# A block of exact row maxima as a short loop, the middle batches written out, and a maximum over partitions taken through TensorE

## The chip, the cores and the metric

The kernel runs on one core of one Trainium2 chip. The metric is the device time in microseconds (us) of one execution. A profile is one further execution, recorded by the hardware profiler; its span runs from the first to the last instruction.

## What is computed

One transformer layer in float32 accuracy: attention with rotary embedding over 4 batches of 1024 tokens with 256 channels and 16 heads of 16, then a mixture of 8 experts of which each token uses 2. Cut to what matters here:

```python
x = x + attn(layernorm(x))        # B=4, L=1024, E=256, H=16, HD=16
#   q, k = rope(x @ Wq.T + bq), rope(x @ Wk.T + bk);  v = x @ Wv.T + bv
#   softmax(q k^T / 4) v @ Wo.T + bo
x = x + ffn(layernorm(x))
#   nf = rmsnorm(x) in bf16; top 2 of 8 logits, softmax over the two
#   p1 = nf @ mlp1; act = min(g,7) * sigmoid(1.702 g) * (clip(lin)+1)
#   combined = sum over experts of weight * (act @ mlp2)
```

The softmax needs protection from overflow. The kernel bounds every score of a batch by the largest norm of a query times the largest norm of a key. If the bound is small, the exponential is taken without a shift. If it is large, a block of code first computes the exact maximum of each row of scores and the shift is the negative of that. With the inputs used here the bound stays small: in the profile the block is jumped over in each of the 4 batches.

## The kernel before

The kernel is written for the five engines by hand: each engine has its own instruction stream, and semaphores join them. An engine's sequencer reads the stream, does branches, waits and register arithmetic itself and queues the rest. PE is TensorE, DVE is VectorE, ACT is ScalarE, POOL is GpSimd, SP is SyncE, which here only issues DMAs.

Work is cut into 4 batches (`b`), each of 2 chunks (`n`) of 512 query tokens. A chunk of attention is 32 steps (`s`): 4 groups of 4 heads (`g`) times 8 tiles of 128 keys (`kt`). A step is two pairs of score matmuls into `S` (line 673), two exponentials on ACT into `probs` (line 804) and 4 pairs of matmuls into `OP` (line 687). The scores of the next step are issued before the values of this one, but not across the end of a batch.

Other work is put beside the steps by a table of due times in half steps: `PREP` prepares the next batch's chunk (normalisation `stats1`, `xn`; transposes `xT`; projections `qk`, `v`; rotation; the squared norms `length`), `POST` finishes the attention of the chunk before and does the gating, `EXPERTS` does 16 half experts (`up`, `tanh`, `hidden`, `down`). Most TensorE work of the table goes through the one PSUM bank `D`: a stage in the list `FILLS` waits until the reader of the bank's last content has read it (`read_of`), fills the bank and counts `d_full`; the reader then waits for that count. `down` uses the same bank and waits in the same manner.

Per batch there is one check of the bound. `length` leaves maxima over tokens in `nsq` (line 970). At half step 36 of the second chunk stage `guard` runs: DVE reduces `nsq` to `nsq2`, one value per partition for queries and one for keys (line 974), and POOL takes their maxima over the 128 partitions into `nsqa` by `partition_all_reduce` (line 868). At half step 44 stage `flag` multiplies the two and writes `exact_flag` (lines 977 and 979). For batch 0 the same happens in a head, before any attention, with the stages in the order of a list, `HEAD`, and with four PSUM banks in turn.

Between batches each of SP, PE and DVE runs `turn(b)`: it waits for the flag, loads it into a register (lines 426, 706, 1153), and jumps over the exact block if it is 0 (lines 511, 707, 1154) and then over nothing at a second branch (lines 524, 727, 1166), behind which semaphores are set that the block would have set. On PE the block is 128 score groups written out, each a wait and two matmuls with their weight loads; on DVE it is 128 pairs of a wait and a reduction. On PE `turn` ends with the first scores of the batch. On SP in front of it, in the last step of the batch, stand the seven loads of a group's `Qs` and `Ks`, and behind it, in step 0, the load of the next `X` (line 438), that of `X1s` (line 447) and the write of `O`. In batch 0 `turn` itself issues 14 loads of `Qs` and `Ks`.

The batches: `body(0)` is written out, batches 1 and 2 are the two passes of a hardware loop over one code, `body(3)` is written out, then a tail without attention. ACT issues the load of an expert's weights (line 796) once per expert, behind a `tanh`, so the starts of line 796 mark how far the table has come.

## Time and profile before

| | us |
|---|---|
| median of 3 runs | 1203.12 |
| lowest, highest | 1199.26, 1204.91 |
| profiled execution | 1205.98 |
| its span | 1204.1 |
| its mean granted TensorE clock | 0.906 of full speed |

In the rows of the trace a time in square brackets is the idle time of the engine ahead of the instruction and what ended it; "issue" there means that the profile shows nothing the engine waited for. A name with a q (PEldq, SPq) is an engine's sequencer. MODIFY_POOL_CONFIG is an instruction that `partition_all_reduce` brings along, as does the first ordinary POOL operation behind it.

### The profile page before, as it was taken

The numbers are of one execution on the slowest core, as the hardware profiler recorded it, in microseconds if no ns is written. First come the engines' busy times: TensorE is split into PE (matmuls) and PEld (weight loads), VectorE is DVE, ScalarE is ACT, GpSimd is POOL, SyncE is SP. The second block draws the span as 40 slices with busy tenths as digits, with TensorE's granted clock in tenths as the row PEclk, the third lists the DMA queues.
The fourth block names the chain that finished last, engine by engine and source line by source line (L and its number), as shares of the span: only waits on it lengthen the run. The fifth ranks groups of instructions, "written<-read, shape, count | busy, mean of one in ns | idle before, by whom it ended". The sixth has DMA issues, their size and how long they took to land.

```text
span 1204.1 us, 18696 instructions
## 1 busy us (share of the span) xinstructions
PE 974.9 (81%) x5241; PEld 414.1 (34%) x5313; DVE 828.1 (69%) x1622; ACT 697.5 (58%) x905; POOL 424.8 (35%) x360
## 2 busy tenths in 40 slices
PE   4608897889679897987778997888799999996564
PEld 1302222233233443333233343323343344344243
DVE  5732102669658797677676799586867897797797
ACT  2318895856448574765448665675567676771232
POOL 2413303433244333533235333542232333233243
PEclk9858998989889999988799898999989899997587
DMA  4254454324424252434413345352534353421011
GB/s 150 74 108 79 102 104 99 88 74 97 116 59 130 77 117 82 102 96 95 119 37 103 98 108 118 71 128 67 114 86 107 97 125 82 101 76 58 31 53 31
DMA packets 80001, 110.08 MB, mean 91 GB/s; under 512 B 22523, under 2 KB 56707, under 8 KB 76803
## 3 DMA queue, kind: packets, MB, share of 16 engines
q1 hardware_dynamic: 61444, 83.47, 29.9%
q10 hardware_dynamic: 18432, 25.17, 7.0%
q8 instruction: 52, 0.85, 0.3%
q14 instruction: 73, 0.59, 0.2%
HBM read 82.89 MB, written 25.69 MB: 90 GB/s over the span
## 4 chain that ended last, share of the span: by engine, by line
PE 49%; DVE 25%; issue 13%; ACT 4%; DMA 3%; POOL 2%; SPq 2%; another core or an unknown queue 1%; DVEq 0%; ACTq 0%; POOLq 0%
PE OP L687 13%; PE S L673 12%; PE D L659 8%; DVE th_sb L1103 3%; DVE act_sb L1108 3%; PE A L642 3%; PE D L569 3%; PE D L586 3%; PE BB L642 3%; DVE acc L1098 2%; DVE g_sb L1086 2%; DVE l_sb L1088 2%; DMA X<-in_x 2%; DVE xn L946 2%; ACT probs L804 2%
## 5 line engine op out<-in xcount | busy, mean ns | idle before, releaser
L804 ACT ACTIVATE probs<-S 128x1024 f32<-128x1024 f32 x512 | 511.8, 1022 | 256.2 <-PE S L673 253.4
L673 PE MATMUL S<-Qs,Ks 98*128 98x512 bf16 x1024 | 312.4, 399 | 61.8 <-issue 23.0
L687 PE MATMUL OP<-probs,V 128*17 128x512 f32 x2048 | 280.1, 620 | 2.7 <-ACT O L813 2.7
L891 POOL TENSOR_TENSOR act_lo<-act_sb,act_hi 128x512 fp32r<-128x512 f32 x128 | 165.5, 1293 | 212.3 <-DVE act_hi L1114 152.4
L673 PEld LDWEIGHTS S<-Qs,Ks 98*128 98x128 bf16 x1024 | 81.4, 101 | 249.0 <-ACT probs L804 98.7
L659 PE MATMUL D<-W,act_hi 128*128 128x256 f32 x448 | 135.6, 333 | 29.5 <-DVE Vn L986 16.2
L1098 DVE SCALAR_TENSOR_TENSOR acc<-D,combh,acc 128x256 f32<-128x256 f32 x224 | 97.1, 475 | 82.5 <-PE D L659 82.1
L1103 DVE SCALAR_TENSOR_TENSOR th_sb<-th_sb,g_sb 128x512 f32<-128x512 f32 x128 | 129.6, 1012 | 0.7 <-ACT th_sb L780 0.7
L885 POOL TENSOR_SCALAR W<-W2b 128x512 fp32r<-128x512 bf16 x64 | 45.4, 709 | 217.4 <-PE D L659 212.1
L1108 DVE SCALAR_TENSOR_TENSOR act_sb<-l_sb,th_sb 128x512 f32<-128x512 f32 x128 | 107.2, 837 | 16.7 <-POOL act_lo L891 12.2
L659 PE MATMUL D<-W,act_lo 128*128 128x256 f32 x448 | 116.3, 290 | 0.0
L780 ACT ACTIVATE th_sb<-g_sb 128x512 f32<-128x512 f32 x128 | 80.0, 625 | 51.4 <-DVE g_sb L1086 50.7
L659 PEld LDWEIGHTS D<-W,act_hi 128*128 128x128 f32 x448 | 88.5, 198 | 56.4 <-issue 24.7
L642 PE MATMUL A<-nfT,W 128*128 128x512 bf16 x185 | 66.2, 418 | 34.5 <-DVE g_sb L1086 24.9
L1086 DVE TENSOR_SCALAR g_sb<-A,b1f 128x512 f32<-128x512 f32 x120 | 89.3, 744 | 4.2 <-PE A L642 4.2
L659 PEld LDWEIGHTS D<-W,act_lo 128*128 128x128 f32 x448 | 89.0, 199 | 2.3
L1088 DVE TENSOR_SCALAR l_sb<-BB,b1f 128x512 f32<-128x512 f32 x120 | 89.0, 742 | 0.5
L642 PE MATMUL BB<-nfT,W 128*128 128x512 bf16 x239 | 77.6, 408 | 0.4
L687 PEld LDWEIGHTS OP<-probs,V 128*17 128x17 f32 x2048 | 34.3, 96 | 116.5 <-issue 87.2
L569 PE MATMUL D<-xnT,wqk_sb 128*128 128x512 f32 x108 | 53.4, 618 | 11.4 <-DVE acc L1098 8.3
L858 POOL TENSOR_TENSOR sw<-sw,sin_sb 128x512 f32<-128x512 f32 x32 | 43.2, 1349 | 49.0 <-DVE sw L953 48.9
L1114 DVE CAST act_hi<-act_sb 128x512 fp32r<-128x512 f32 x112 | 51.7, 461 | 4.2
(136 smaller groups left out, 1016.7 us busy)
## 6 DMA issues: line engine op xcount, KB each, us to landing
W<-in_w ACTq DMA_DIRECT2D x64, 256.0 KB, 2.7
Ks<-k_scr SPq DMA_DIRECT2D x32, 384.0 KB
W2b<-in_w ACTq DMA_DIRECT2D x64, 128.0 KB, 2.7
Ks<-k_scr SPq DMA_DIRECT2D x32, 256.0 KB
o_scr<-O SPq DMA_DIRECT2D x32, 256.0 KB, 4.5
q_scr<-parts SPq DMA_DIRECT2D x16, 384.0 KB, 3.1
k_scr<-parts SPq DMA_DIRECT2D x16, 384.0 KB, 2.6
Qs<-q_scr SPq DMA_DIRECT2D x32, 192.0 KB
```

The source lines that it names most:

```text
L569: last = mm(bank[:, :], wqk_sb[:, c, P * a:P * (a + 1)], xnT[:, c, :], start=c == 0, stop=c == CT - 1)
L642: last = mm(bank, W1[:, e % 2, c, FI * gl + P * it:FI * gl + P * (it + 1)], nfT[:, c, :], start=c == 0, stop=c == CT - 1)
L659: last = mm(bank[:, E * q:E * (q + 1)], part[:, e % 2, it, tok:tok + P], W2[:, e % 2, E * it:E * (it + 1)], start=k == 0, stop=k == 3)
L673: last = mm(S[:, j2, C * i:C * (i + 1)], Ks[0:SROWS + MROWS, g % 2, j, P * kt:P * (kt + 1)], Qs[0:SROWS + MROWS, g % 2, j, :], start=True, ...
L687: last = mm(OP[32 * j:32 * j + VW, :], V[:, kt, HG * g + j, :], probs[:, s % 2, C * j:C * (j + 1)], start=kt == 0, stop=kt == KT - 1)
L804: nc.scalar.activation(probs[:, s % 2, 2 * C * j2:2 * C * (j2 + 1)], S[:, j2, :], ACT.Exp, scale=SCALE).then_inc(exp_done, 1)
L891: tt(act_lo[:, e % 2, it, :], act_sb[:, a % 2, :], act_hi[:, e % 2, it, :].bitcast(FP32), ALU.subtract).then_inc(lo_s, 1)
L1086: v.tensor_scalar(g_sb[:, q, :], gate, b1f[:, e, 0, it:it + 1], LIMIT, ALU.add, ALU.min).then_inc(g_s, 1)
L1088: v.tensor_scalar(l_sb[:, q, :], linear, b1f[:, e, 1, it:it + 1], 1.0 - LIMIT, ALU.add, ALU.max).then_inc(l_s, 1)
L1098: v.scalar_tensor_tensor(acc[:, t, :], output[:, E * i:E * (i + 1)], combh[:, t, e:e + 1], acc[:, t, :], ALU.mult, ALU.add).then_inc(m2_ev, 1)
L1103: v.scalar_tensor_tensor(th_sb[:, q, :], th_sb[:, q, :], 1.0, g_sb[:, q, :], ALU.add, ALU.mult).then_inc(t1_s, 1)
L1108: v.scalar_tensor_tensor(act_sb[:, q, :], l_sb[:, q, :], 1.0 + LIMIT, th_sb[:, q, :], ALU.min, ALU.mult).then_inc(act_s, 1)
```

## The change

Three things. The exact block becomes loops in registers: on PE one loop of 4 passes for each group of heads, on DVE one of 16 passes for each chunk; the matmuls take their operands at an address from the loop's register. Batches 1 and 2 are written out instead of being passes of a hardware loop. The maximum over partitions is taken by two TensorE transposes of `nsq2` into the first row of a bank and one DVE reduction of 256 values: stage `gmax` (half step 36) holds the old DVE part of `guard`, `guard` moves to half step 39 and becomes a filling of the bank, `flag` moves from 44 to 41. `nsqa`, `bound` and `exact_flag` shrink to one partition.

```diff
-          "qk3": 30, ..., "v1": 42, "guard": 1, "flag": 8, ...
+          "qk3": 30, ..., "v1": 42, "gmax": 1, "guard": 4, "flag": 6, ...
-    place(PREP, h + AT["length"] + AT["guard"], ("guard", 0))
-    place(PREP, h + AT["length"] + AT["guard"] + AT["flag"], ("flag", 0))
+    for st in ("gmax", "guard", "flag"):
+        place(PREP, h + AT["length"] + AT[st], (st, 0))
-    HEAD += [("guard", 0, 1), ("flag", 0, 1)]
+    HEAD += [("gmax", 0, 1), ("guard", 0, 1), ("flag", 0, 1)]
-    FILLS = ("xT", "qk", "v", "length", "wo", "nfT", "logits", "combT", "b2")
+    FILLS = ("xT", "qk", "v", "length", "guard", "wo", "nfT", "logits", "combT", "b2")
...
             body(0, True, FILLED0)
-            with engine.Fori(1, B - 1) as b:
+            for b in range(1, B - 1):
                 body(b, True, FILLED1 + LOOP_FILLS * (b - 1))
             body(B - 1, False, FILLED3)
...
 # PE, read_of
+                        "guard": (nsqa_s, u // NCH + 1), ...
 # PE, stage
+                elif st == "guard" and n == NCH - 1:
+                    pe.wait_ge(nsq_s, bb + 1)
+                    for t in range(2):
+                        last = nc.tensor.transpose(bank[0:1, P * t:P * (t + 1)], nsq2[:, t:t + 1], ident[:, :])
+                    last.then_inc(d_full, 1)
 # PE, turn
-                            for j in range(HG):
+                            with pe.Fori(0, HG) as j:
                                 for t in range(TC):
-                                    i = 16 * (NG * n + g) + TC * j + t
-                                    if i >= 2:
-                                        wait_apart(pe, (ex_red, 128 * b + i - 1))
+                                    wait_apart(pe, (ex_red, 128 * b + 16 * (NG * n + g) + t + 1 + TC * j))
                                     for hf in range(2):
-                                        last = mm(S[:, i % 2, C * hf:C * (hf + 1)], Qs[0:SROWS, g % 2, j, P * t:P * (t + 1)],
-                                                  Ks[0:SROWS, g % 2, j, C * hf:C * (hf + 1)], start=True, stop=True)
+                                        last = mm(S[:, t % 2, C * hf:C * (hf + 1)],
+                                                  Qs[0:SROWS, g % 2, bass.ds(j, 1), P * t:P * (t + 1)].rearrange("k o t -> k (o t)"),
+                                                  Ks[0:SROWS, g % 2, bass.ds(j, 1), C * hf:C * (hf + 1)].rearrange("k o t -> k (o t)"),
+                                                  start=True, stop=True)
                                     last.then_inc(ex_mm, 1)
-                    wait_apart(pe, (ex_red, 128 * (b + 1)))
+                    wait_apart(pe, (ex_red, 128 * (b + 1) + 1))
 # POOL, stage
-                elif st == "guard" and n == NCH - 1:
-                    wait_apart(pool, (nsq_s, bb + 1))
-                    nc.gpsimd.partition_all_reduce(nsqa[:, :], nsq2[:, :], P, bass.bass_isa.ReduceOp.max).then_inc(nsqa_s, 1)
 # DVE, stage
-                elif st == "guard" and n == NCH - 1:
+                elif st == "gmax" and n == NCH - 1:
                     dve.wait_ge(nrm_red, 4 * (u + 1))
                     v.reduce_max(nsq2[:, :], nsq[:, :, :], AX_X).then_inc(nsq_s, 1)
+                elif st == "guard" and n == NCH - 1:
+                    dve.wait_ge(d_full, k + 1)
+                    v.reduce_max(nsqa[:, :], bank[0:1, 0:2 * P].rearrange("o (a p) -> o a p", a=2), AX_X).then_inc(nsqa_s, 1)
 # DVE, turn
-                    for i in range(128):
-                        n, g, j, t = i // 64, i // 16 % NG, i // TC % HG, i % TC
-                        wait_apart(dve, (ex_mm, 128 * b + i + 1))
-                        h = HG * g + j
-                        v.reduce_max(mx[:, TC * n + t, h:h + 1], S[:, i % 2, :], AX_X).then_inc(ex_red, 1)
+                    for n in range(NCH):
+                        with dve.Fori(0, H) as h:
+                            for t in range(TC):
+                                wait_apart(dve, (ex_mm, 128 * b + 64 * n + t + 1 + TC * h))
+                                v.reduce_max(mx[:, TC * n + t, bass.ds(h, 1)], S[:, t % 2, :], AX_X).then_inc(ex_red, 1)
```

The remaining lines count the fillings of bank `D` with one more per batch and start the semaphore `ex_red` at 1, so that the first waits of the loop have a positive value.

## Rows read from the trace of the kernel before

**Rows 1.** Page, parts 1, 3 and 4: engines; instruction fetches; chain by engine.
```profile
PE 974.9 (81%) x5241; PEld 414.1 (34%) x5313; DVE 828.1 (69%) x1622; ACT 697.5 (58%) x905; POOL 424.8 (35%) x360
...
q8 instruction: 52, 0.85, 0.3%
...
PE 49%; DVE 25%; issue 13%; ACT 4%; DMA 3%; POOL 2%; SPq 2%; another core or an unknown queue 1%; DVEq 0%; ACTq 0%; POOLq 0%
```

**Rows 2.** Chain in order of time, end of the head: start us, us, what.
```profile
68.82 5.82 issue
...
75.42 0.02 SPq L345
```

**Rows 3.** Line 345, waits on their own, 68 to 72 us: engine, count, ns, first to last start.
```profile
L345 SPq EVENT_SEMAPHORE  x2: 17/17/17, 69.0 to 71.1; - x2
```

**Rows 4.** Timeline around the check of batch 1's bound: start, us, engine, line, idle before.
```profile
260.29 0.37 POOL L868 PARTITION_ALL_REDUCE nsqa<-nsq  x1 [11.31 <-issue]
...
267.50 1.26 POOL L891 TENSOR_TENSOR act_lo<-act_sb,act_hi 128x512 fp32r<-128x512 f32 x1 [6.83 <-issue]
...
268.90 1.00 DVE L1108 SCALAR_TENSOR_TENSOR act_sb<-l_sb,th_sb 128x512 f32<-128x512 f32 x1 [3.26 <-POOL act_lo L891]
```

**Rows 5.** Line 796 in four stretches; the last two numbers are first and last start.
```profile
L796 ACTq DMA_DIRECT2D W<-in_w x3: 339/339/339, 403.8 to 426.0; - x3
L796 ACTq DMA_DIRECT2D W<-in_w x3: 334/334/334, 258.4 to 285.0; - x3
L796 ACTq DMA_DIRECT2D W<-in_w x3: 339/339/340, 536.1 to 565.7; - x3
L796 ACTq DMA_DIRECT2D W<-in_w x3: 339/339/339, 818.8 to 845.8; - x3
```

**Rows 6.** Lines 563 and 970, whole execution: count, ns least/median/most.
```profile
L563 PE MATMUL D<-ident,xn x52: 272/418/476, 9.9 to 753.0; 128*128 128x128 f32 x52
L970 DVE TENSOR_REDUCE nsq<-D x24: 684/692/693, 114.1 to 812.2; 128x1 f32<-128x512 f32 x24
```

**Rows 7.** Branches on the sequencers: count, ns least/median/most, first to last start.
```profile
L707 PEldq COMPARE_BRANCH  x4: 3901/6237/8002, 76.4 to 865.8; - x4
L377 PEldq COMPARE_BRANCH  x2: 76/2698/5320, 591.6 to 874.2; - x2
L1154 DVEq COMPARE_BRANCH  x4: 56/63/67, 76.4 to 868.5; - x4
L1166 DVEq COMPARE_BRANCH  x4: 55/55/55, 79.5 to 876.5; - x4
L511 SPq COMPARE_BRANCH  x4: 50/52/64, 76.4 to 869.9; - x4
```

**Rows 8.** Timeline at the three turns between batches, first scores, and DVE behind them.
```profile
313.72 1.86 PE L673 MATMUL S<-Qs,Ks 98*128 98x512 bf16 x4 [7.41 <-issue]
...
318.82 0.88 DVE L1098 SCALAR_TENSOR_TENSOR acc<-D,combh,acc 128x256 f32<-128x256 f32 x2 [10.09 <-PE D L659]
...
591.51 1.88 PE L673 MATMUL S<-Qs,Ks 98*128 98x512 bf16 x4 [4.66 <-issue]
...
597.13 1.03 PE L673 MATMUL S<-Qs,Ks 98*128 98x512 bf16 x2 [3.74 <-issue]
...
874.05 1.89 PE L673 MATMUL S<-Qs,Ks 98*128 98x512 bf16 x4 [7.17 <-issue]
```

**Rows 9.** Timeline, load of X behind the first and second turn and its first use.
```profile
310.04 0.43 SPq L438 DMA_DIRECT2D X<-in_x  x1
...
323.79 1.40 DVE L918 BATCH_NORM_STATS2 st<-X 128x6 f32<-128x256 f32 x4
...
596.30 0.43 SPq L438 DMA_DIRECT2D X<-in_x  x1
...
604.98 1.39 DVE L918 BATCH_NORM_STATS2 st<-X 128x6 f32<-128x256 f32 x4
```

**Rows 10.** Chain in order of time between the chunks of batch 1.
```profile
447.63 8.38 DMA X<-in_x
```

More of the change, by code:

```diff
@@ L127, in block_kernel @@
             HEAD += [("sum", *tile[0])]
-    HEAD += [("guard", 0, 1), ("flag", 0, 1)]
+    HEAD += [("gmax", 0, 1), ("guard", 0, 1), ("flag", 0, 1)]
     HEAD_BANKS = 4
-    FILLS = ("xT", "qk", "v", "length", "wo", "nfT", "logits", "combT", "b2")
-    PREP_FILLS = sum(st in FILLS for l in PREP.values() for st, _ in l)
+    FILLS = ("xT", "qk", "v", "length", "guard", "wo", "nfT", "logits", "combT", "b2")
+    PREP_FILLS = sum(st in FILLS and st != "guard" for l in PREP.values() for st, _ in l)
     POST_FILLS = sum(st in FILLS for l in POST.values() for st, _ in l)
@@ L159, in stages @@
                 k = (self.n, self.last, False)
-                if st in FILLS:
+                if st in FILLS and (st != "guard" or chunk == NCH - 1):
                     self.n, self.last = self.n + 1, (st, a, NCH * batch + chunk)
@@ L270, in block_kernel @@
         nsq2 = sb("nsq2", [P, 2], FP32)
-        nsqa = sb("nsqa", [P, 2], FP32)
-        bound = sb("bound", [P, 1], FP32)
-        exact_flag = sb("exact_flag", [P, B], INT32)
+        nsqa = sb("nsqa", [1, 2], FP32)
+        bound = sb("bound", [1, 1], FP32)
+        exact_flag = sb("exact_flag", [1, B], INT32)
         lgb = sb("lgb", [P, TC, NE], BF16)
@@ L345, in wait_apart @@
                 engine.sem_inc(passed, 1)
-        FILLED0 = NCH * PREP_FILLS
-        FILLED1 = FILLED0 + NCH * PREP_FILLS + POST_FILLS
-        LOOP_FILLS = NCH * (PREP_FILLS + POST_FILLS)
+        FILLED0 = NCH * PREP_FILLS + 1
+        FILLED1 = FILLED0 + NCH * PREP_FILLS + 1 + POST_FILLS
+        LOOP_FILLS = NCH * (PREP_FILLS + POST_FILLS) + 1
         FILLED3 = FILLED1 + 2 * LOOP_FILLS
@@ L547, in read_of @@
                 return {"xT": (xnT_s, 2 * u + a + 1), "qk": (qk_b, 4 * u + a + 1), "length": (nrm_red, 4 * u + a + 1),
-                        "v": (vn_s, 2 * u + a + 1), "wo": (x1_s, 2 * u + a + 1), "nfT": (nfT_s, u + 1),
+                        "guard": (nsqa_s, u // NCH + 1), "v": (vn_s, 2 * u + a + 1), "wo": (x1_s, 2 * u + a + 1), "nfT": (nfT_s, u + 1),
                         "down": (m2_ev, 2 * (NF * u + a + 1)), "logits": (gating, GATING * u + 1), "combT": (combT_s, u + 1), "b2": (acc_s, 2 * u + a + 1)}[st]
@@ L553, in stage @@
                 u = NCH * bb + n
-                if st in FILLS and filling[1]:
+                if st in FILLS and filling[1] and (st != "guard" or n == NCH - 1):
                     pe.wait_ge(*read_of(*filling[1]))
@@ L1168, in turn @@
                     dve.sem_inc(ex_red, 128)
+            dve.sem_inc(ex_red, 1)
             v.memset(half_pow[:, :], -0.5).then_inc(c_set, 1)
```

4 rows, old and new, of the table AT are left out of this document.

## The prediction

> **What bounds the kernel now.** Read the page first. TensorE is busy 81% of the span and the chain that ended last lies on it for 49%, on DVE for 25%; 13% is "issue", time in which an engine stood still and the profile shows no work that it waited for [rows 1]. An 81% busy engine with a chain that hops to DVE is no place for large gains by less work, so the 13% is where to look. The change touches three places, and each is a stall of this kind. The chain in order of time shows the first, at the end of the head: 5.82 us of "issue", from 68.82 on, ahead of the maximum over partitions [rows 2]. The timeline shows the same in the check of each later batch's bound, only in the middle of running work: POOL is still for 11.31 us ahead of its 0.37 us instruction and for another 6.83 us behind it, and DVE and then TensorE come to stand behind POOL [rows 4]. The third place is the turn from one batch to the next: TensorE idle ahead of the first scores by 7.41, 4.66 and 7.17 us, and a second time by 3.74 us behind the second turn, where the hardware loop goes back to its start [rows 8]. The branch over the exact block alone takes the PE sequencer between 3.90 and 8.00 us, the loop's branch back 5.32 us; a branch that goes nowhere far takes 0.08 (the least of line 377) [rows 7]. TensorE's granted clock needs no term of its own: the idle times above are what changes, and what a slower clock does behind a stall lies inside the stretches measured next.
>
> **Part 1, the head.** Now: POOL has its input and begins 5.82 us of standing still at 68.82, and SP sees the flag at 75.42 [rows 2]. After: two transposes on an idle TensorE, 0.27 to 0.48 us each [rows 6], and a DVE reduction of 256 values where 512 take 0.69 [rows 6], so 0 to 0.69, taken as 0.45. From 68.7: 0.7 + 0.45 + some 0.1 us for each of four hand-overs, and the two small flag operations, which with the maximum itself lie within the 75.42 - 74.64 = 0.8 us between the end of the standing still and SP now, taken as 0.35; the flag would be ready near 70.6. SP is then not free: its two waits for the last writes of keys and queries run at 69.0 and 71.1, each passed in 0.017 us when it ran, and the second began only when the first had been met and SP came free again at 71.1 [rows 3]. I read this as the write landing at about 71. So SP goes on near 71.2 in place of 75.4. All else of batch 0 hangs on SP's loads behind it. Gain 4.2; with the new operations at twice my price 3.2; it cannot pass 4.3.
>
> **Part 2, the check of the bound in batches 1 to 3.** Line 796 is a clock of the table. From the load issued in step 19 to the second one after it the first chunk of batch 1, which has the same work without the check, takes 426.0 - 403.8 = 22.2 us. With the check it is 26.6, 29.6 and 27.0 us [rows 5]. So the checks cost 4.4 + 7.4 + 4.8 = 16.6 us. What comes in: on PE two transposes, 0.54 to 0.96 us, and the wait for `down`'s reader ahead of them; on DVE the reduction, up to 0.69; behind them the next `down` waits for `nsqa_s`. On DVE the new reduction stands behind a `down` and a `hidden` and ahead of an `up`, so the next `down` on PE starts late by what DVE has left of `hidden`, under 1 us (its operation in the rows took 1.00 while POOL held it [rows 4]). On the queues: behind `guard` on PE stand the next `up`, scores and `down`; POOL loses its only part and then has nothing in these steps that it does late. Per check 0.3 to 2.5 us; I take 1.0, nearest to two transposes plus a short wait. Net 16.6 - 3.0 = 13.6, range 9 to 15.7. `flag` moves three half steps forward, which SP's wait in step 23 never notices.
>
> A rule speaks against this part. The Trainium skill, GPSIMD Engine Reference, § 4.1 Engine selection, names GPSIMD as the engine for a reduction along the partition dimension. This trace shows a cheap instruction between two expensive stalls, so the row and the rule differ on what is to be counted; the rule's outcome is the fourth case below.
>
> **Part 3, the turns.** The idle times that could go are 7.41, 4.66 + 3.74 and 7.17 [rows 8]. Three things decide.
>
> First, whether PE's jump becomes short. 52 instruction fetches served 5241 matmuls and 5313 weight loads [rows 1], 203 per fetch, and somewhat more since the sequencer's own instructions are not in that count and since some fetches were of code jumped over: 203 to 260 instructions per fetched block. From the code the exact block on PE is 128 x (1 wait + 2 x 2) + some 26 = 666 instructions, about 3 blocks: always outside. SP's block at line 511 is some 80 to 200 instructions and its branch costs 0.05 us four times out of four [rows 7]. So I assume that the block after the current one is there and nothing beyond. After the change PE's exact block is, per group, four times (a wait with its register operation, 4 matmul and load instructions, 2 to 4 register operations for addresses) and some 5 for loop and load wait, 37 to 45 instructions, times 8, plus 20: 316 to 380, or 1.2 to 1.9 fetched blocks. The chance that the landing point is in the next one is 2 minus that length, 0.1 to 0.8; I take 0.6, for each of three turns on its own. The first of the four jumps, in the head, is under SP's loads either way.
>
> Second, DVE. It goes the same way at present: 3.1 us at the first turn and 8.0 at the last between its first and second branch [rows 7]. Its block falls from 256 instructions to some 45 and fits, so DVE no longer arrives with TensorE. If it did not fit, it would take TensorE's place: `acc` waits for PE today at 318.82 [rows 8] and would then wait for DVE itself.
>
> Third, SP. In the first and second turn SP issues the next `X` only behind its seven loads and the turn, at 310.04 and 596.30; DVE first reads it at 323.79 and 604.98 [rows 9]. Between the chunks of batch 1, where DVE waits for it, the load takes 8.38 us [rows 10]. At that price `X` would be there at 318.4 in the first turn: 5.4 us can be won before DVE waits for it, up to 7.4 if the load lands sooner. I take 5.8. In the second turn SP's own way back to the loop's start falls away, an estimate of 4.2 us from PE's 5.32, `X` is issued near 592.1 and is there at 600.5: 4.5 to 8.1, taken as 5.3. The third turn loads no `X`: 7.17, less a little for the chain of `O`, 6.9. Sum 18.0 if all three jumps fit. A jump that does not costs 3.9 to 8.0 [rows 7]; of the gain it takes back about 5.5.
>
> Written-out code besides: the check's stretch of batch 0's pass, which is written out today, and that of the loop's second pass take 26.6 and 27.0 us [rows 5]. Nothing to gain or lose in the steady part. More code is fetched in sequence, as the written-out batches are today.
>
> A rule bears on the jumps. The Trainium skill, Runtime: NRT & Kernel Launch, § Instruction fetch mechanics, says that a taken branch to outside the current window of two pages stalls for a fetch, and it gives TensorE 2048 instructions of room. The first half agrees with the rows; the second would have let PE's present jump of 666 instructions pass for nothing, and the rows show 3.90 us at the least. If the room is that large after all, all three new jumps fit, which is the second case.
>
> **The sum.** With two of three jumps inside: 4.2 + 13.6 + (18.0 - 5.5) = 30.3. The profiled execution took 1205.98 us, 1.9 more than its span; 1205.98 - 30.3 = 1175.7. The median of the runs lies 2.9 below the profiled execution, and I set the new median as far below: 1172.8.
>
> **The cases.**
> 1. As above, one jump of three still outside: 1172.8. Chance 0.41.
> 2. All three inside: 1172.8 - 5.5 = 1167.3. For it: SP's jump never misses. Against: length near one and a half blocks. 0.22.
> 3. None or one inside. Then 5.5 or 11 us more than case 1, 1178.3 to 1183.8; what stays is the head, the checks and the way back of the loop. For it: if addresses take more register operations than I count, the block nears two fetches. 0.28.
> 4. The way through bank `D` costs what POOL's stall did. DVE has work queued and `guard` on PE waits for a reader, then `down` waits for `guard`'s: two hand-overs per check. At 4 us a check instead of 1 the gain falls by 9 to 1181.8. Against: of the stretch in question POOL's stall fills all, and DVE is idle there for 3.26 us. 0.06.
> 5. Slower. The written-out middle runs slower than the loop: each of its four chunks would have to lose more than (30.3 + 6) / 4 = 9.1 us, by fetches in sequence that the loop spares. The pair 26.6 and 27.0 speaks against any loss. It would give 1209 or more. 0.02.
> The last 0.01 is left to what I don't see.
>
> The range: low end case 2 with the checks at 15.7, 1165, and a little for the first turn, 1163; high end within case 3 and over case 4, 1184. This measurement can tell 0.5%, 6 us, from no change: faster by more 0.96, within 0.02, slower 0.02.
>
> **What would show it.** Head: SP's flag wait at 71.2 in place of 75.4; if later, the new operations are dear. Checks: the stretches of line 796 at about 23 us, and no MODIFY_POOL_CONFIG beyond the first operations; 26 would be case 4. Turns: branches of line 707 at under 0.2 us, or again at 4 to 8; no branch at line 377 at all; DVE idle ahead of `BATCH_NORM_STATS2` on the load of `X` in the first two turns. I am wrong if PE's idle time at the turns stays above 4 us although its branch is short, or if TensorE's stretches of equal work are longer in batches 1 and 2 than before.

## The result and the profile after

The changed kernel takes 1153.45 us, the median of 4 runs (1152.27 to 1154.23), against 1204.01 us for the kernel before in the same session (4 runs, 1199.26 to 1205.35). The ratio is 0.9593, with a 95% interval of 0.9562 to 0.9624: 50.6 us or 4% faster. The forecast was 1172.8, range 1163 to 1184. The direction was right, the gain was forecast at 30.3 us, and the time lies 10 us below the low end of the range. The profiled execution of the changed kernel took 1154.16 us, its span 1152.4; against the 1205.98 of the recording before that is 51.8 us less. The mean granted TensorE clock rose from 0.906 to 0.937.

The page of the changed kernel, parts 1, 3 and 4, answers to [rows 1]:

```profile
PE 965.9 (84%) x5320; PEld 407.3 (35%) x5320; DVE 826.8 (72%) x1625; ACT 695.2 (60%) x905; POOL 424.9 (37%) x356
...
q8 instruction: 47, 0.77, 0.3%
q14 instruction: 48, 0.39, 0.1%
...
PE 45%; DVE 26%; issue 9%; DMA 7%; ACT 5%; SPq 4%; POOL 2%; ACTq 1%; DVEq 0%; POOLq 0%
```

No engine's work changed much: TensorE is busy for 965.9 us where it was for 974.9. "Issue" in the chain fell from 13% to 9%, 157 to 104 us. That is as much as the whole gain, but the shares do not show where the gain lies: in the same views TensorE's part of the chain fell by 71 us and the parts of DMA and SP grew by 45 and 22 (each known to some 12 us, since the shares are whole per cents). TensorE's busy time fell by 9 us although two transposes per batch came in; this goes with the higher granted clock.

**The head.** The chain in order of time of the changed kernel, and its line 345 from 66 to 73 us (engine, count, ns, first to last start), answer to [rows 2, 3]:

```profile
68.44 2.52 DMA k_scr<-parts
...
71.19 0.47 SPq L426
```

```profile
L345 SPq EVENT_SEMAPHORE  x4: 17/17/17, 68.9 to 71.1; - x4
```

POOL's standing still is gone from the chain, and what is late now is the write of the keys: SP goes on at 71.19. Its branch over the block, at 76.4 before [rows 7], runs at 72.02 (4.4 us earlier).

**The checks.** The start of each expert's weight load, line 801 now, in the four stretches of [rows 5] in order of time (batch 0's pass, the first chunk of batch 1 without a check, and the passes of batches 1 and 2 with one):

```profile
L801 ACTq DMA_DIRECT2D W<-in_w x3: 334/334/335, 252.4 to 275.4; - x3
L801 ACTq DMA_DIRECT2D W<-in_w x3: 334/335/335, 385.7 to 408.1; - x3
L801 ACTq DMA_DIRECT2D W<-in_w x3: 334/335/341, 518.7 to 541.4; - x3
L801 ACTq DMA_DIRECT2D W<-in_w x3: 334/334/334, 784.3 to 807.3; - x3
```

With the check they take 23.0, 22.7 and 23.0 us where they took 26.6, 29.6 and 27.0, so 14.5 us are gone, and without it 22.4 (22.2 before). A check now costs 0.3 to 0.6 us in these stretches. The timeline around one (start, us, engine, line, idle before) shows why:

```profile
255.05 0.38 PE L578 MATMUL D<-ident,nsq 128*1 128x128 f32 x2
...
256.31 0.40 DVE L979 TENSOR_REDUCE nsqa<-D 1x2 f32<-1x256 f32 x1
...
256.76 0.19 PEld L664 LDWEIGHTS D<-W,act_hi 128*128 128x128 f32 x1 [0.53 <-DVE nsqa L979]
```

The two transposes take 0.38 us together and the reduction 0.40. `down` behind them waits for 0.53 us; POOL is not in the picture.

**The turns.** The branches over the block (line 712 on PE, 1159 and then 1171 on DVE: ns least/median/most), and PE's timeline at the first turn, answer to [rows 7, 8]:

```profile
L712 PEldq COMPARE_BRANCH  x4: 316/340/3321, 71.0 to 827.4; - x4
...
L1159 DVEq COMPARE_BRANCH  x4: 56/60/67, 71.0 to 830.1; - x4
...
L1171 DVEq COMPARE_BRANCH  x4: 50/50/55, 71.3 to 830.3; - x4
```

```profile
296.60 1.03 PE L678 MATMUL S<-Qs,Ks 98*128 98x512 bf16 x4
298.31 0.61 PE L678 MATMUL S<-Qs,Ks 98*128 98x512 bf16 x2 [0.69 <-ACT probs L809]
...
300.25 1.05 PE L692 MATMUL OP<-probs,V 128*17 128x512 f32 x8
```

All three jumps between batches fit (0.32 to 0.35 us; the 3.3 us are the one in the head, under SP's loads). The first scores have no idle time ahead of them, and they take 1.03 us for four matmuls where they took 1.86 [rows 8]. This is the first sign of what the forecast left out: TensorE was slow behind the stall too. From the first scores to the first values of the batch it is 3.65 us. The cost of a whole turn is read from four weight loads, from the last but one ahead of the turn to the second behind it; first three lines before, then three after:

```profile
L796 ACTq DMA_DIRECT2D W<-in_w x4: 339/344/396, 303.7 to 387.7; - x4
L796 ACTq DMA_DIRECT2D W<-in_w x4: 339/340/396, 584.3 to 668.3; - x4
L796 ACTq DMA_DIRECT2D W<-in_w x4: 334/336/339, 864.3 to 929.0; - x4
```

```profile
L801 ACTq DMA_DIRECT2D W<-in_w x4: 334/335/342, 294.1 to 370.0; - x4
L801 ACTq DMA_DIRECT2D W<-in_w x4: 334/334/338, 560.1 to 635.7; - x4
L801 ACTq DMA_DIRECT2D W<-in_w x4: 334/334/351, 826.1 to 882.2; - x4
```

84.0, 84.0 and 64.7 us became 75.9, 75.6 and 56.1: gains of 8.1, 8.4 and 8.6, in sum 25.1. The load of `X` and its first use, as in [rows 9]:

```profile
300.27 0.41 SPq L438 DMA_DIRECT2D X<-in_x  x1
...
306.94 1.41 DVE L920 BATCH_NORM_STATS2 st<-X 128x6 f32<-128x256 f32 x4 [1.97 <-DMA X<-in_x]
...
572.22 1.41 DVE L920 BATCH_NORM_STATS2 st<-X 128x6 f32<-128x256 f32 x4 [1.28 <-DMA X<-in_x]
```

As forecast, DVE now waits for `X` in the first two turns, for 1.97 and 1.28 us.

### The profile page after: what moved, and what is told of

It is laid out like the page before. It is cut to its first block, busy times and chain, and to the rows that moved or that the text cites. A ratio compares the mean times of both kernels' runs of the same rounds, so it can differ in the third digit from the quotient of the medians.

```text
span 1152.4 us, 16694 instructions
## 1 busy us (share of the span) xinstructions
PE 965.9 (84%) x5320; PEld 407.3 (35%) x5320; DVE 826.8 (72%) x1625; ACT 695.2 (60%) x905; POOL 424.9 (37%) x356
## 4 chain that ended last, share of the span: by engine, by line
PE 45%; DVE 26%; issue 9%; DMA 7%; ACT 5%; SPq 4%; POOL 2%; ACTq 1%; DVEq 0%; POOLq 0%
PE OP L692 12%; PE S L678 11%; PE D L664 6%; DVE th_sb L1108 4%; DMA X<-in_x 4%; PE D L569 3%; DVE act_sb L1113 3%; PE A L647 3%; PE D L591 3%; DVE acc L1103 3%; PE BB L647 3%; DVE g_sb L1091 2%; ACT probs L809 2%; DVE l_sb L1093 2%; DVE xn L948 2%
## 5 line engine op out<-in xcount | busy, mean ns | idle before, releaser
L678 PE MATMUL S<-Qs,Ks 98*128 98x512 bf16 x1024 | 303.6, 389 | 30.7 <-DMA Qs<-m_scr 15.3
L692 PE MATMUL OP<-probs,V 128*17 128x512 f32 x2048 | 275.2, 610 | 2.7 <-ACT O L818 2.7
L664 PE MATMUL D<-W,act_hi 128*128 128x256 f32 x448 | 130.5, 324 | 22.4 <-DVE acc L1103 12.8
L664 PE MATMUL D<-W,act_lo 128*128 128x256 f32 x448 | 112.5, 283 | 0.0
L785 ACT ACTIVATE th_sb<-g_sb 128x512 f32<-128x512 f32 x128 | 80.1, 626 | 52.2 <-DVE g_sb L1091 50.9
L664 PEld LDWEIGHTS D<-W,act_hi 128*128 128x128 f32 x448 | 85.3, 190 | 50.4 <-DVE acc L1103 17.6
L647 PE MATMUL A<-nfT,W 128*128 128x512 bf16 x240 | 78.0, 409 | 27.1 <-DVE g_sb L1091 27.1
L664 PEld LDWEIGHTS D<-W,act_lo 128*128 128x128 f32 x448 | 85.6, 191 | 2.0
L647 PE MATMUL BB<-nfT,W 128*128 128x512 bf16 x240 | 75.9, 400 | 0.4
L861 POOL TENSOR_TENSOR rot<-qb,cos_sb 128x512 f32<-128x512 f32 x24 | 32.9, 1370 | 63.4 <-ACT qb L755 63.4
```

What stands on the lines that cost most here:

```text
L647: last = mm(bank, W1[:, e % 2, c, FI * gl + P * it:FI * gl + P * (it + 1)], nfT[:, c, :], start=c == 0, stop=c == CT - 1)
L664: last = mm(bank[:, E * q:E * (q + 1)], part[:, e % 2, it, tok:tok + P], W2[:, e % 2, E * it:E * (it + 1)], start=k == 0, stop=k == 3)
L678: last = mm(S[:, j2, C * i:C * (i + 1)], Ks[0:SROWS + MROWS, g % 2, j, P * kt:P * (kt + 1)], Qs[0:SROWS + MROWS, g % 2, j, :], start=True, ...
L692: last = mm(OP[32 * j:32 * j + VW, :], V[:, kt, HG * g + j, :], probs[:, s % 2, C * j:C * (j + 1)], start=kt == 0, stop=kt == KT - 1)
```

## The experiments

Times are medians of 4 runs, with the ratio to the kernel before of the same session and its 95% interval, unless said otherwise. The kernel before has medians from 1199.9 to 1204.0 us in the four sessions, so a difference of two medians from different sessions is known to some 4 us only. Each is the changed kernel with what the diff shows, but for the second recording of the kernel before.

### The maximum over partitions back on POOL

```diff
-    FILLS = ("xT", "qk", "v", "length", "guard", "wo", ...)
+    FILLS = ("xT", "qk", "v", "length", "wo", ...)
+ # POOL, stage guard, behind gmax
+     nc.gpsimd.partition_all_reduce(nsqa[:, :], nsq2[:, :], P, bass.bass_isa.ReduceOp.max).then_inc(nsqa_s, 1)
```

> The changed kernel with the maximum over partitions taken back to POOL (stage at half step 37, flag at 44), all else as changed. If each part is worth what the line-796 stretches of the changed kernel show against those of before (head 4.3 us, checks 14.5 us inside the stretches), this kernel is 19 us slower than the changed one, near 1172. If the slow clock behind each stall of POOL also costs at the places where the changed kernel gained without having been changed (1.6 and 1.1 us ahead of two checks, 2 to 3 us elsewhere), it is 22 to 25 us slower, near 1177. If the stall was half hidden by something else that is now late, under 12 us, below 1165.

1178.24 us, ratio 0.9802 (0.9766 to 0.9838): 24.8 us over the changed kernel. The head in the chain, POOL at the first check, and the first stretch of line 796 (its line here):

```profile
66.93 6.44 issue
```

```profile
259.87 0.51 POOL L868 PARTITION_ALL_REDUCE nsqa<-nsq  x1 [10.30 <-issue]
267.69 1.26 POOL L891 TENSOR_TENSOR act_lo<-act_sb,act_hi 128x512 fp32r<-128x512 f32 x1 [7.31 <-issue]
```

```profile
L796 ACTq DMA_DIRECT2D W<-in_w x3: 334/334/334, 257.3 to 286.5; - x3
```

The three stretches with a check take 29.2, 28.7 and 27.3 us, 16.5 more than in the changed kernel; SP loads the flag in the head at 74.28 in place of 71.19, 3.1 us later. Of the other 3.8 us of the profiled difference (23.4), 1.9 lie in batch 0 ahead of the first check and 1.5 ahead of the second, both with more half-speed time of TensorE than in the changed kernel. So this part is worth 16.5 + 3.1 by the places where it acts and up to 24.8 by the medians; the forecast had 13.6 + 4.2 = 17.8.

### Both blocks written out again

```diff
-                            with pe.Fori(0, HG) as j:
+                            for j in range(HG):
...
-                        with dve.Fori(0, H) as h:
+                    for i in range(128):
```

> The changed kernel with the exact block written out again on PE and on DVE (666 and some 260 instructions), all else as changed. Theory 1, a turn costs TensorE's idle time and nothing more, and X's load hides part of it: three jumps of 4 to 8 us, of which 3 x 5.5 = 17 us reach the end: 1170. Theory 2, a turn costs its idle time and the half-speed clock behind it, and X's load hides nothing (the turns gained 8.0, 8.3 and 8.7 us in the changed kernel): 1153.5 + 22 to 25 = 1177. Its trace should show granted half speed for some 10 us behind each turn, which the changed kernel does not have there.

1182.62 us, ratio 0.984 (0.9789 to 0.989): 29.2 us over the changed kernel. The four times spread from 1175.18 to 1185.21; the profiled execution is 25.9 us over that of the changed kernel, and by the weight loads its three turns are 7.1, 9.2 and 8.8 us longer, 25.0 together. PE's branches and the first turn:

```profile
L712 PEldq COMPARE_BRANCH  x4: 3761/7408/7917, 69.2 to 845.1; - x4
```

```profile
303.99 1.86 PE L678 MATMUL S<-Qs,Ks 98*128 98x512 bf16 x4 [6.78 <-issue]
...
309.66 0.71 PE L692 MATMUL OP<-probs,V 128*17 128x512 f32 x4
```

The idle time is 6.78, 7.30 and 6.69 us at the three turns, and behind it the way from the first scores to the first values takes 5.67 us (309.66 - 303.99), 2.0 more than in the changed kernel; at the other two turns it takes 4.0 and 2.0 more. Idle time alone is 20.8 us, and the slow way behind it 8.0. Against both stand the 3.3 us that the changed kernel waits for `X` and this one does not: 20.8 + 8.0 - 3.3 = 25.5, beside the 25.0 of the weight loads. The time lies above both theories' numbers; the half-speed stretches behind the turns are those of theory 2.

### The same, with TensorE kept at work during the jump

Twelve float32 matmuls without use stand ahead of the flag's wait, on top of the edit above:

```diff
+                if not (isinstance(b, int) and b == 0):
+                    for i in range(12):
+                        mm(S[:, i % 2, C * (i // 2 % 2):C * (i // 2 % 2 + 1)], ident[:, :], xnT[:, 0, :], start=True, stop=True)
                 wait_apart(pe, (flag_s, b + 1))
```

> The changed kernel with both exact blocks written out again, so that the jump on PE costs 7.4 to 7.9 us as in the run with the long blocks alone, and with 12 float32 matmuls without use into S ahead of the flag's wait in the turns behind batches 0 to 2. They keep TensorE at work while its sequencer jumps (some 0.5 us each at full clock, 6 us in all). Nothing of the computation is left out. Theory (behind a jump TensorE runs at half its clock, and this costs some 2 us per turn on top of the idle time): no half-speed stretch begins between the jump and 10 us behind it, from the first scores of the new batch to its first complete pair of value matmuls takes 3.7 us as in the changed kernel and not 5.7 us, and the whole lies 4 to 7 us below the run with the long blocks (1182.6), near 1177. Rival (the half-speed stretches come at their own times, whatever TensorE does at the turn): the half-speed stretch is still there, the time is 1182 or more.

1181.32 us, ratio 0.982 (0.9791 to 0.9849). The mechanism came out as the theory has it, the time did not. The matmuls took 10.46 us in the first turn and not the 6 I had priced, so that the first scores wait for them and not for the jump. The timeline of the first turn, and windows of 14 us around and behind the first scores (busy time and count of PE, PEld, DVE, ACT, POOL, then the granted clock, the DMA share and GB/s): the kernel before, the one above, and this one at its three turns:

```profile
298.61 10.46 PE L712 MATMUL S<-xnT,ident 128*128 128x512 f32 x24
309.00 1.02 PE L678 MATMUL S<-Qs,Ks 98*128 98x512 bf16 x4
```

```profile
311.00:325.00 14.00, 10.78 (x51) 4.98 (x52) 6.01 (x11) 7.51 (x9) 1.85 (x2) 0.70 0.50 122
```

```profile
303.00:317.00 14.00, 12.75 (x63) 5.43 (x64) 8.01 (x19) 8.90 (x10) 2.97 (x4) 0.75 0.52 134
```

```profile
309.00:323.00 14.00, 13.15 (x84) 5.90 (x84) 10.52 (x22) 9.71 (x11) 5.11 (x5) 1.00 0.21 62
583.00:597.00 14.00, 13.16 (x76) 6.00 (x77) 9.03 (x20) 9.27 (x11) 4.03 (x4) 1.00 0.28 87
857.00:871.00 14.00, 13.15 (x78) 6.14 (x78) 8.69 (x14) 9.60 (x12) 3.13 (x3) 1.00 0.15 44
```

With the engine idle through the jump the clock behind it is 0.70 and 0.75, a mean of the two levels of 2.4 and 1.2 GHz; with the engine at work it stays at 1.00 in all three turns, and from the first scores to the first values it is 3.65, 3.64 and 3.65 us, as in the changed kernel. PE's branches are shorter here, 6.33, 4.88 and 5.26 us, and end before the filler does. At the first turn the useful work stood still for 10.4 us in place of 6.8, 3.6 longer, and the turn by the weight loads was only 0.8 us longer (83.7 against 82.9). So 2.8 us came back with the clock. The rival, that the slow stretches come at their own times, is out. The time was forecast near 1177 and is hardly lower than without the filler, since I had priced the filler wrong; in this form it wins nothing.

### The block written out on PE alone

> The changed kernel with the exact block written out on PE alone (DVE keeps its two loops). Theory (TensorE's jump is all that costs in the turns): PE's three branches over the block take 7 to 8 us each, DVE's 0.06, and the time is that of both blocks written out, 1178 to 1183. Rival (with both blocks written out the two engines' jumps add up, PE's first and then DVE's): 3 us or more per turn below that, 1172 or less.

1181.48 us, ratio 0.9832 (0.9803 to 0.986), with branches of 8.10, 7.98 and 7.98 us on PE and 0.06 on DVE. That is the time of both blocks written out, so beside PE's long jump DVE's long jump costs nothing that can be told. The page has 50 instruction fetches on queue 8 here and 48 on queue 14; the changed kernel has 47 and 48.

### The block written out on DVE alone

> The changed kernel with the exact block written out on DVE alone (256 instructions there; PE keeps its loops). Theory of the prediction (if DVE's block did not fit it would take TensorE's place): DVE stands 3 to 8 us between its first and second branch in at least one of the three turns and the time is 3 to 15 us above the changed kernel, 1156 to 1168. Rival (a jump over 256 instructions fits, or DVE has work queued that covers it): within 2 us of the changed kernel, 1151 to 1156.

1166.17 us, ratio 0.9695 (0.9666 to 0.9724): 12.7 us over the changed kernel. PE's branches are short (0.32 to 0.34 us), and DVE at the first and second turn:

```profile
304.43 0.88 DVE L1103 SCALAR_TENSOR_TENSOR acc<-D,combh,acc 128x256 f32<-128x256 f32 x2 [6.55 <-issue]
...
572.00 0.88 DVE L1103 SCALAR_TENSOR_TENSOR acc<-D,combh,acc 128x256 f32<-128x256 f32 x2 [5.22 <-issue]
```

Between DVE's two branches stand 3.1 us in the head and 7.1, 5.8 and 7.1 at the turns, where the changed kernel has 0.2. The point of the prediction holds: a jump over some 260 instructions does not fit on DVE (four of four miss), and it takes TensorE's place once PE's fits. By the weight loads the three turns are 3.0, 1.4 and 2.4 us longer than in the changed kernel; most of the rest of the 12.7 is in half-speed stretches away from the turns, such as twice 3.2 us in batch 3. By the medians PE's loop alone brings 1182.6 - 1166.2 = 16.4 of the 29.2 us.

Why does DVE miss a jump over some 260 instructions, where PE takes one over 290 three times out of three? The page of this kernel, part 3, tells:

```profile
q8 instruction: 47, 0.77, 0.3%
q14 instruction: 55, 0.44, 0.2%
```

Writing out PE's block changed the fetches on queue 8 alone, writing out DVE's those on queue 14 alone (48 in the changed kernel). A fetch on queue 8, PE's, brings 0.77 MB / 47 = 16 KB, and one on queue 14, DVE's, 0.44 / 55 = 8 KB. If an instruction takes the same bytes on both, a fetched block of 256 instructions on PE (the longer blocks further on bear this number out) is one of 128 on DVE. This is an estimate from the sizes; no run has a block on DVE of a length in between. A jump over some 260 is then longer than two blocks of DVE and goes past the next one from every place.

### Batches 1 and 2 as passes of a hardware loop

```diff
-            for b in range(1, B - 1):
+            with engine.Fori(1, B - 1) as b:
```

> The changed kernel with batches 1 and 2 as two passes of a hardware loop again, the exact block short. The prediction priced the way back of the loop at some 3.4 us through TensorE's second stall of the second turn, and nothing in the steady part: 1157. If the loop's registers and waits cost in the steady part as well (two half batches each), it is 8 us or more: 1162 and above. If fetches behind the way back collide with the loads of X, up to 6 us.

1162.84 us, ratio 0.9694 (0.9656 to 0.9732): 9.4 us over the changed kernel, where 1157 was forecast and 1162 was the number of the rival. PE at the second turn:

```profile
564.48 1.03 PE L678 MATMUL S<-Qs,Ks 98*128 98x512 bf16 x4
571.55 0.13 PEld L678 LDWEIGHTS S<-Qs,Ks 98*128 98x128 bf16 x2 [6.53 <-ACT probs L809]
```

Between the first scores and the next stands the branch back of line 377, which takes 6.73 us here and ends at 571.38. The releaser named, ACT's exponential, is hardly earlier: ACT goes back to the loop's start too, stands still for 5.98 us, and its two exponentials end at 571.00. So without PE's way back ACT's would hold the turn. By the weight loads the second turn is 5.5 us longer (81.1 against 75.6). Most of the rest are 2.0 us in the first chunk of batch 1 and 2.0 in that of batch 2, where TensorE ran at half speed for longer; the next experiment but one shows such differences between two recordings of one kernel. So the size is the rival's, but its reason, a cost in the steady part, is hardly seen: the stretches with a check take 23.4 and 23.4 us in batches 1 and 2 against 22.7 and 23.0, 1.0 us together.

### Loop and written-out blocks together

> The changed kernel with two parts undone together: both exact blocks written out, and batches 1 and 2 as the two passes of a hardware loop. Each alone costs 29.2 us (1182.6) and 9.4 us (1162.8) over the changed kernel's 1153.5. Theory (in the second turn the two jumps of PE do not add up: in the kernel before, both together leave it idle there for 8.4 us, each alone for 7.3 and 6.0 us; so what the loop's way back adds to a turn that is late anyway is small): 1177 to 1185, about that of the long blocks alone. Rival (the parts add up): 1153.5 + 29.2 + 9.4 = 1192, at the least 1188.

1180.82 us, ratio 0.985 (0.9825 to 0.9875): 27.4 us over the changed kernel, not the 38.6 that the two parts cost one at a time. PE at the second turn:

```profile
575.37 1.88 PE L678 MATMUL S<-Qs,Ks 98*128 98x512 bf16 x4 [5.48 <-issue]
580.76 1.03 PE L678 MATMUL S<-Qs,Ks 98*128 98x512 bf16 x2 [3.51 <-issue]
```

The two waits are 9.0 us together; alone they are 7.3 and 6.0. With the blocks written out, the loop costs nothing that can be told (1180.8 against 1182.6). The loop's 9.4 us could be won only because the blocks became short as well. In this split the parts add up within what can be told: 27.4 for the jumps and 24.8 for POOL's maximum are 52.2, and 50.6 was measured (by the ratios of each session 56 and 49).

### The kernel before, recorded a second time

> The kernel before, unchanged, profiled a second time. Theory (half-speed stretches of TensorE far from the three places of the change come by chance): the stretches right behind the three turns (8 to 14 us long) are there again, but the intervals between weight loads 24 and 25 and between 40 and 41, 2.0 and 3.2 us longer before than after, come out 2 us or more apart from the first recording in at least one of the two. Rival: both intervals repeat within 0.5 us; then these 5 us belong to the change.

One run, 1201.46 us. The interval between the two weight loads in the middle of batch 3 from 929 us on (882 us in the changed kernel), far from all that the change touches, in the first recording, the second, and the changed kernel:

```profile
L796 ACTq DMA_DIRECT2D W<-in_w x2: 334/334/335, 929.0 to 942.4; - x2
```

```profile
L796 ACTq DMA_DIRECT2D W<-in_w x2: 334/334/335, 929.5 to 939.7; - x2
```

```profile
L801 ACTq DMA_DIRECT2D W<-in_w x2: 334/342/351, 882.2 to 892.4; - x2
```

The same kernel takes 13.4 us here once and 10.2 the other time; the granted clock around it is 0.79 and 1.00. In the first chunk of batch 2 another such interval is 17.75 and 16.10 us. Behind the second turn, from 592 to 606 us, the clock is low both times, 0.62 and 0.68. Behind the first and third turn, too, both recordings have a half-speed stretch of 10.2 us that begins during the stall. So the slow stretches behind the stalls come with the kernel, and those away from them by chance, as far as two recordings tell.

### A longer block on PE, by 110, 220 and 330 instructions

Waits of one instruction each that are never executed lengthen PE's block, which counts some 290 instructions in the listing, to some 400, 510 and 620:

```diff
+                    for _ in range(110):
+                        wait_apart(pe, (ex_ld[0], EX_STACK * (4 * b + 1)))
                     wait_apart(pe, (ex_red, 128 * (b + 1) + 1))
```

> The changed kernel with 110 waits more (one instruction each, never executed) in PE's exact block, which counts some 290 instructions now: 400. Theory 1 (what can be reached without a stall is the fetched block of 256 instructions after the current one): one or two of the three turns' branches over the block take 4 to 8 us, the others 0.3, and the time is 1160 to 1175. Theory 2 (the room is larger, the written-out block's 666 instructions are just over it): all three at 0.3 us, 1152 to 1156.

> As the kernel with 110 waits more, with 220: 510 instructions. Theory 1: all three branches 4 to 8 us, 1175 to 1183. Theory 2: all three 0.3 us, 1152 to 1156.

> As the kernel with 110 waits more, with 330: 620 instructions. Theory 1: all three branches 4 to 8 us, 1175 to 1183. Theory 2: at least one branch still at 0.3 us and the time under 1172.

One run each: 1174.62, 1176.51 and 1178.54 us. Line 712 in the three kernels, in this order (ns least/median/most of four, the head's among them):

```profile
L712 PEldq COMPARE_BRANCH  x4: 432/5760/8098, 70.5 to 835.3; - x4
```

```profile
L712 PEldq COMPARE_BRANCH  x4: 3881/7770/8697, 71.4 to 838.3; - x4
```

```profile
L712 PEldq COMPARE_BRANCH  x4: 3534/7785/8247, 70.2 to 839.5; - x4
```

At 290 instructions none of three jumps between batches is missed, at 400 two are (8.10 and 7.84 us, the other 0.43), at 510 and 620 all three. Theory 1 holds, and the rival, that the room is larger, is out. The places of the branches in the compiled program say the same more sharply. If PE's blocks are 256 instructions long and a jump is short exactly when it lands in the block it starts from or in the next, then one common offset of the blocks (41 to 45 instructions ahead of the first) gives every short and every missed jump of PE in the kernel before, the changed one, the one with the loop, the one with both blocks written out and these three, the misses in the head included. Blocks of 128 or 512 give them with no offset. So a jump over some 290 instructions is short from about seven places in eight; the one in the head stands in the eighth.

### X loaded earlier

The load of `X` for the next chunk moves from step 0 of that chunk to the last step of the one before, ahead of the seven loads and the turn:

```diff
+                elif st == "x_in" and not (early or u <= NCH):
+                    pass
...
                 if aside is not None and kt == KT - 1:
+                    if g == NG - 1 and NCH * b + n + 1 + NCH < NCH * B:
+                        stage("x_in", 0, *divmod(NCH * b + n + 1 + NCH, NCH), (0, None, True), early=True)
```

> The changed kernel with X loaded ahead of the seven loads of the last step in place of behind them, from the second chunk of batch 0 on. In the changed kernel DVE waits for X in five stretches behind the start of a chunk (2.0 us in the first turn, about as much or more in the others). Theory, the wait stands on the path: 5 x 2 to 4 us, so 10 to 18 us faster, 1136 to 1144. Rival, X's wait only lets other work go first and PE is as late with the other stages: within 3 us of 1153.

1144.18 us, ratio 0.9518 (0.9488 to 0.9547): the fastest of all, 9.3 us below the changed kernel, a little less than the 10 to 18 of the theory. The load and its first use around the first turn:

```profile
286.52 0.42 SPq L440 DMA_DIRECT2D X<-in_x  x1
...
300.81 1.40 DVE L924 BATCH_NORM_STATS2 st<-X 128x6 f32<-128x256 f32 x4
```

Ahead of the other loads it lands within 3.7 to 3.9 us, where it took 6.1 to 9.6 behind them (6.7 and 6.1 at the first two turns), and DVE no longer waits. By the weight loads 2.3 us go at the first turn, 2.1 between the chunks of batch 1, 2.3 at the second turn and 1.0 between the chunks of batch 2, 7.7 together; batch 0, whose second chunk also gets its `X` earlier, is 5.5 us shorter as well, but this batch takes from 222 to 228 us up to its first check in the other variants of the changed kernel, so that cannot be put down to `X`. So `X` did limit the turns as the prediction said; it only limited them less.

## Why the prediction was wrong

The sum was made against the profiled execution, 30.3 us; 51.8 were measured there. Step by step:

- **The head: right.** 4.2 forecast, 4.4 by SP's branch. What is late next is the keys' write at about 71, as read from [rows 3].
- **The checks: right, a little small.** 13.6 forecast, 14.5 against the first recording and 15.6 against the second (its stretches take 27.6, 27.6 and 29.1 us). The price of a check was set at 1.0 us and is 0.3 to 0.6. The 11.31 us of POOL in [rows 4] were read as one stall; MODIFY_POOL_CONFIG starts at 254.5, so 5.8 of them are behind it, and before that POOL waits for DVE's maxima. The sum does not use the 11.31. The fourth case, the way through bank `D` as dear as POOL, is out. The Trainium skill (GPSIMD Engine Reference, § 4.1 Engine selection) names GPSIMD for a reduction along the partition dimension; here that way took 24.8 us more than two transposes and a reduction of 0.40 us.
- **How many jumps fit: the first step that failed, 5.5 us.** The mechanism held on PE, the block after the current one and nothing beyond. The length was mis-sized: 316 to 380 instructions by my count of register operations, some 290 in the listing. With 400 instructions two of three jumps miss and with 290 none, so the likeliest case was picked by this count. Case 2 came true, at a chance of 0.22; by the prediction's own rule 290 instructions are 1.13 blocks, which gives 0.87 for each jump and 0.66 for all three. The 3.1 us that Part 3 gives for DVE's first turn are those of the head; the first turn has 7.0.
- **TensorE's clock: the step that failed in kind.** "TensorE's granted clock needs no term of its own" was wrong. I took the idle times as all that would go. But behind each of the three stalls TensorE ran at half its clock (0.70 from 311 to 325 us, at the first), and the written-out blocks with and without a filler show that this follows from the idle time: 5.67 against 3.65 us from the first scores to the first values. In the kernel before the same way takes 5.68, 5.42 (without the second stall) and 5.39 us, so the term put at nothing is 2.0 + 1.8 + 1.7 = 5.5 us. Part of [rows 8] said so already: the first four matmuls of a batch take 1.86 to 1.89 us there, and the same four 1.03 a few steps on (at 881.30 us behind the third turn).
- **The wait for X: right at the first turn, mis-sized at the second.** By taking 5.8 of 7.41 and 5.3 of 8.40 us the sum left 1.6 and 3.1 us of wait for `X`; 1.97 and 1.28 were measured. The load was taken at 8.38 us, from [rows 10], and took 6.7 and 6.1. Together this is 1.5 us.
- **The turns as a whole.** The gains are 8.1, 8.4 and 8.6 us, 25.1 against the 18.0 of the case in which all jumps fit. What the three turns lost and kept gives this number: 23.0 us of idle time gone (all of [rows 8]), 5.5 of slow clock gone, 3.3 of wait for `X` come in, 25.2.
- **The written-out middle: right in the steady part.** The stretch without a check (22.4 against 22.2) shows neither gain nor loss. The fifth case is out.
- **What is left.** 51.8 - 4.4 - 14.5 - 25.1 = 7.8 us. Of these, 1.6 lie ahead of the first check (an interval of 17.4 us before and 15.8 after; it is 17.4 as well with both blocks written out again and with `X` loaded earlier, so this too is chance). The largest others are 3.2 in batch 3, 2.0 in batch 2 and 1.9 in the tail, and the second recording has neither the 3.2 nor the 1.9 and 1.65 less of the 2.0. They are half-speed stretches by chance, in a recording of before that was 2.0 us above the median of its session. Three intervals of the table (from 241, 388 and 668 us on in the kernel before) take 15.7 to 16.1 us in some of the kernels here and 17.2 to 17.8 in the others, whatever was changed. Against the second recording the whole is 47.3 us: 4.4, 15.6 and 25.4 (7.5, 10.1 and 7.8 for the turns) leave 1.9.

The range held all three jumps inside and the checks at 15.7, so the count of the jumps moved the forecast but did not break the range. The clock did, with the wait for `X` and what chance gave. Case 2 with the turns at 25.1 would have been 1167.3 - 7.1 = 1160.2, still 6.7 us above the measured time: the head and the checks are 1.1 of these and the 7.8 us of what is left the rest, less 2.2 us because the median after lies 0.7 and not 2.9 below its profiled execution. What is left is chance for the most part, and it made the miss larger. An unknown that is priced at nothing belongs at least in the range.

What stays open: why the branch over the written-out block takes 5.0 to 7.5 us in the second and third turns of the kernels with a loop, 4.9 to 6.3 with the filler in front, and 7.4 to 8.1 otherwise; and what decides when TensorE's clock falls away from the stalls.

## What to carry to other kernels

A branch over a rare block costs by the block's length in instructions, not by its work: count the listing, keep the block under one fetched block (256 instructions on PE here, 128 on DVE by the estimate from its fetches), and do so on every engine that jumps, since the longest stall hides the others and each part undone alone tells a wrong sum. When a stall of some microseconds goes, add what TensorE loses behind it at half clock, here 2 us on 7; it can be read from the duration of the same matmul group just behind a stall and elsewhere. And a load that stands behind a burst of others in its queue landed here in 6.1 to 9.6 us instead of 3.7 to 3.9: issue first what is needed first.

## What the runs showed of the hardware that I had not expected

- **A missed jump of PE takes 7.4 to 8.7 us between batches in the kernels without a loop and without a filler, but 3.3 to 4.0 us in the head,** where the short block's jump of some 290 instructions misses too (3.32 us in the changed kernel; 3.76 with the block written out). A single fetch of PE takes some 1 us (47 packets are 0.3% of 16 engines' span of 1152 us), so it does not explain either time; the cause stays open. The head's is hidden by SP's loads, so this costs nothing here.
- **A jump of PE reaches into the next fetched block and no further, and DVE's blocks are half as large.** The Trainium skill (Runtime: NRT & Kernel Launch, § Instruction fetch mechanics) says that blocks of 256 instructions are fetched in sequence and that a branch out of a window of two such pages stalls; what PE's jumps of 290, 400 and 510 instructions do agrees with that, but on DVE the trace has fetches of 8 KB where PE's are 16 KB, and the jump over some 260 instructions misses four times out of four; there too the measurement decides. The same section gives TensorE room for 2048 instructions. The measurement decides: jumps over 510 instructions stall there each time, for 7.4 to 8.7 us between batches.
- **POOL's reduction stalls on both sides.** 10.30 us ahead of it and 7.31 behind it, for an instruction of 0.51 us, at the first check with the maximum back on POOL. Not all of the 10.30 is the stall: MODIFY_POOL_CONFIG runs at 254.1 to 254.2, and 5.7 us lie between it and the reduction at 259.87; before it POOL waits for its input. At all four such instructions of that kernel it is 5.6 to 6.4 us, 23 of the 41.8 us that POOL is idle ahead of them.
